# A second layer whose transposed onehot is compared from broadcast bytes, and gathers held to two groups in advance

## The reference

```
h = relu(layernorm(x))
x = x + segment_sum(h[src] @ weight[edge_type], dst)          # 16 edge types
h = relu(layernorm(x))
m = relu(concat(h[src], h[dst], edge_attr) @ W1 + b1) @ W2 + b2
x = x + segment_sum(m, dst)
```

## Time and profile before

| | |
|---|---|
| median of 3 runs | 5361.71 us (5358.94 to 5369.75) |
| the profiled execution | 5379.53 us, span 5377.8 us |
| mean granted clock of TensorE | 0.705 of 2.4 GHz |
| instructions | 53533 |

### The profile page before, as it was taken

The page is one execution under the profiler, slowest core; times in us unless marked ns, Lnnn a source line. Parts: engine busy times, 40 slices in busy tenths (PEclk is TensorE's granted clock), DMA queues, the critical chain, the costliest instruction groups (busy, mean ns, idle before and its releaser), DMA issues.

```text
span 5377.8 us, 53533 instructions
## 1 busy us (share of the span) xinstructions
PE 3005.4 (56%) x16541; PEld 2352.7 (44%) x16541; DVE 1166.7 (22%) x1424; ACT 742.7 (14%) x1550; POOL 3158.4 (59%) x3348
## 2 busy tenths in 40 slices
PE   2455555555555555555455566566556555565666
PEld 1333333333333333333345555455455555554555
DVE  5222222222222222222311111111111111111111
ACT  2111111111111111111111111111111111111111
POOL 7665665666666665665455555555555555555554
PEclk9677667676776776777767766666676777666667
DMA  4111111111111111111111111111111111111111
GB/s 94 22 25 22 24 25 22 24 25 23 24 25 23 25 23 23 25 24 23 23 24 27 27 27 27 26 27 26 26 27 26 28 27 27 26 27 26 26 28 24
DMA packets 248095, 144.20 MB, mean 27 GB/s; under 512 B 178526, under 2 KB 194199, under 8 KB 248071
## 3 DMA queue, kind: packets, MB, share of 16 engines
q0 software_dynamic: 106496, 109.26, 11.4%
q1 hardware_dynamic: 138949, 34.02, 3.1%
q10 hardware_dynamic: 2626, 0.63, 0.1%
HBM read 129.98 MB, written 12.83 MB: 27 GB/s over the span
## 4 chain that ended last, share of the span: by engine, by line
PE 44%; issue 32%; another core or an unknown queue 21%; DVE 1%; ACT 1%; SPq 1%; DVEq 0%; ACTq 0%; DMA 0%
PE ps L1278 9%; PE ps L1270 9%; PE ps L1202 7%; PE ps L1209 7%; PE ps L1261 4%; PE ps L1268 3%; PE ps L1216 2%; PE ps L1176 1%; PE ps L1249 1%; PE ps L1259 1%; ACT slots L803 0%; DVE onehot L977 0%; SPq L530 0%; PE ps L1165 0%
## 5 line engine op out<-in xcount | busy, mean ns | idle before, releaser
L648 POOL DMA_INDIRECT rows<-p_table,idx x1664 | 1569.9, 943 | 1203.1 <-DMA idx<-in_src_dram 655.6
L648 POOL DMA_INDIRECT rows<-h_table,idx x1616 | 1528.2, 946 | 974.3 <-DMA idx<-src_tab 497.5
L1270 PE MATMUL ps<-q_win,onehot_t 128*128 128x64 f32 x3328 | 579.7, 302 | 797.5 <-issue 795.8
L1270 PEld LDWEIGHTS ps<-q_win,onehot_t 128*128 128x128 f32 x3328 | 568.4, 232 | 932.7 <-issue 932.3
L1202 PE MATMUL ps<-onehot,rows 128*64 128x256 f32 x3328 | 709.3, 477 | 317.4 <-issue 310.0
L1209 PE MATMUL ps<-w_types,slots 128*128 128x128 f32 x3328 | 531.2, 316 | 437.1 <-issue 367.8
L1209 PEld LDWEIGHTS ps<-w_types,slots 128*128 128x128 f32 x3328 | 484.2, 226 | 498.1 <-issue 405.7
L1278 PE MATMUL ps<-onehot,relus 128*65 128x128 f32 x3328 | 575.5, 339 | 155.3 <-issue 110.8
L1202 PEld LDWEIGHTS ps<-onehot,rows 128*64 128x64 f32 x3328 | 337.5, 167 | 607.5 <-issue 530.1
L1278 PEld LDWEIGHTS ps<-onehot,relus 128*65 128x65 f32 x3328 | 511.0, 180 | 180.2 <-issue 164.7
L977 DVE TENSOR_TENSOR onehot<-key,ps 128x2048 f32<-128x2048 f32 x209 | 473.0, 2276 | 456.9 <-remote 441.7
(11 more groups left out here) (117 smaller groups left out, 1037.5 us busy)
## 6 DMA issues: line engine op xcount, KB each, us to landing
rows<-p_table,idx POOLq DMA_INDIRECT x1664
rows<-h_table,idx POOLq DMA_INDIRECT x1616
attr<-in_edge_attr_dram SPq DMA_DIRECT2D x209, 32.0 KB
q_win<-q_table SPq DMA_DIRECT2D x208, 32.0 KB
idx<-in_src_dram SPq DMA_DIRECT2D x208, 4.0 KB
idx<-src_tab SPq DMA_DIRECT2D x202, 4.0 KB
p_table<-pq_out SPq DMA_DIRECT2D x25, 120.0 KB
q_table<-pq_out SPq DMA_DIRECT2D x25, 120.0 KB
```

What stands on the lines that cost most here:

```text
L648: pool.indirect_dma_start(rows[:, u, t, :], None, table, bass.IndirectOffsetOnAxis(ap=idx[:, u, t:t + 1], axis=0)).then_inc(s, 16)
L1270: last = pe.matmul(pre_ps[:, u % 2, j * D:(j + 1) * D], onehot_t[:, u % 2, j * P:(j + 1) * P], q_win[:, u % V, :], start=False, stop=(j == ...
```

## The change

*Second layer, the transposed onehot.* Early on, DVE writes the keys of all edges within their group's window as bytes (`key_bytes`, capped at 255), and SP stores them in a DRAM table of 208 rows of 1024 bytes. In the second layer SP reads four rows at a time, broadcast to all 128 partitions (`key_rows`), and DVE compares a row with the partition's own number (`node_f`), which gives `onehot_t` in SBUF. PE's eight transposes and ACT's two copies of a group are gone; the transposed attributes stay.

*Second layer, loads and order.* Attributes come for four groups in one DMA, and `start_row` with its value loads is gone. SP has one wait for a group. `products(k-1)` comes ahead of the turn of group k on PE, and `add_window`, `add_rows` come ahead of the onehots on DVE. Several waits that others imply are left out.

*Both layers, POOL.* A second wait stands before each group's gathers: the sums (first layer) or row additions (second) of the group two back must be done.

```diff
+        key_table = dram("key_table", (G, GE), u8)
...
+            sp.dma_start(key_table.rearrange("(a g) e -> g a e", a=2), key_bytes[:]).then_inc(bytes_stored, 16)
...
+                def load_keys(g, k):
+                    rows_of = key_table[bass.ds(g, B), :].rearrange("(a g) e -> a g e", a=1)
+                    sp.dma_start(key_rows[:, k * B:(k + 1) * B, :], rows_of.broadcast_to([P, B, GE])).then_inc(key_in[k], 16)
+                def load_attr(g, k):
+                    sp.dma_start(attr[:, k * B:(k + 1) * B, :], attr_of(bass.ds(g * GE, B * GE))).then_inc(attr_in[k], 16)
...
+                def groups(it, ahead=2):
+                    for u in range(U):
+                        g = it * U + u
+                        wait_apart(sp, pre_added, AHEAD + g + 1)
+                        if ahead == 2 or ahead == 1 and u < U - 1:
+                            load_idx((g + U) * GE, u)
...
+                        if ahead or u < V:
+                            load_q(g + V, u % V)
+                        if u % B == B - 1 and (ahead or u < B):
+                            k = u // B
+                            load_keys((it + 1) * U + k * B if ahead else 0, k)
...
                         wait_apart(pool, idx_in[u], 16 * (it + 1) if u >= EG else 16 * it)
+                        wait_apart(pool, slots_summed, 2 * AHEAD + 2 * (it * U + u - 1))
...
                         wait_apart(pool, idx_in[u], 16 * (it + 1 + (NIT if u >= EG else NIT - 1)))
+                        wait_apart(pool, pre_added, it * U + u + AHEAD - 1)
...
-                    act.wait_ge(pre_made, AHEAD + g - 1)
                     act.copy(attr_t[0:T * F, b, :], attrt_ps).then_inc(turn_copied, 1)
-                    for half in range(2):
-                        cols = slice(half * 512, (half + 1) * 512)
-                        act.copy(onehot_t[:, b, cols], oht_ps[:, cols]).then_inc(turn_copied, 1)
...
+            dve.tensor_scalar(key_bytes[:].rearrange("g a (j p) -> g a j p", j=T), key1_g.rearrange("g a (p j) -> g a j p", j=T),
+                              float(2 * P - 1), None, ALU.min).then_inc(bytes_made, 1)
...
+                def make_onehots(g, it, u):
+                    dve.tensor_tensor(oh1[:, u % 4], key1[...], iota_ps[...], ALU.is_equal)
+                    if u % B == 0:
+                        dve.wait_ge(key_in[u // B], 16 * (it + 1))
+                    dve.tensor_scalar(onehot_t[:, u % 2, :], key_rows[:, u, :], node_f[:], None, ALU.is_equal).then_inc(onehot1, 1)
...
-                    for j in range(T):
-                        last = pe.transpose(oht_ps[:, j * P:(j + 1) * P], oh1[:, u % 4, j, :], ident[:])
-                    last.then_inc(group_turned, 1)
...
-                    turn_group(k, it, u)
                     if not first or u >= 1:
                         products(k - 1, it if u else it - 1, (u - 1) % U)
+                    turn_attr(it, u)
```

More of the change, by code:

```diff
@@ L38, in gnn_kernel @@
     V = 4
+    B = 4
     NIT = G // U
@@ L110, in gnn_kernel @@
         onehot_t = sb("onehot_t", [P, 2, T * P], fp32)
-        attr = sb("attr", [P, V, T * F], fp32)
+        attr = sb("attr", [P, U, T * F], fp32)
         attr_t = sb("attr_t", [T * F + 1, 2, P], fp32)
@@ L273, in gnn_kernel @@
         q_in = [sem(f"q_in_{u}") for u in range(V)]
-        attr_in = [sem(f"attr_in_{u}") for u in range(V)]
+        attr_in = [sem(f"attr_in_{h}") for h in range(U // B)]
+        key_in = [sem(f"key_in_{h}") for h in range(U // B)]
+        tail_in = sem("tail_in")
         onehot1 = sem("onehot1")
@@ L585, in _ @@
             with sp.If(fits > 0):
[L586 to L591, removed]
-                    base = sp.value_load(base_row[0:1, bass.ds(g, 1)], min_val=0, max_val=N - 1)
[L593 to L610, removed]
-                    for u in range(U):
-                        group(it, u)
-                    store_out(it - 2, chunk_nodes)
+                def attr_of(edges):
+                    return edge_attr[edges, :].rearrange("(g p j) f -> p g (j f)", p=P, j=T)
+                def load_keys(g, k):
+                    rows_of = key_table[bass.ds(g, B), :].rearrange("(a g) e -> a g e", a=1)
+                    sp.dma_start(key_rows[:, k * B:(k + 1) * B, :], rows_of.broadcast_to([P, B, GE])).then_inc(key_in[k], 16)
@@ new lines, in load_attr, with load_last_attr @@
+                def load_attr(g, k):
+                    sp.dma_start(attr[:, k * B:(k + 1) * B, :], attr_of(bass.ds(g * GE, B * GE))).then_inc(attr_in[k], 16)
+                def load_last_attr():
+                    first, k = (G - B) * GE, U // B - 1
+                    sp.dma_start(attr[:, k * B:U - 1, :], attr_of(slice(first, first + (B - 1) * GE))).then_inc(tail_in, 16)
+                    sp.wait_ge(tail_in, 16)
+                    sp.dma_start(attr[:, U - 1:U, :], attr_of(slice(LAST, E))).then_inc(attr_in[k], 16)
@@ new lines, in load_idx, with load_q @@
+                def load_idx(first, u):
+                    sp.dma_start(idx[:, u, :], src[bass.ds(first, GE)].rearrange("(p j) -> p j", j=T)).then_inc(idx_in[u], 16)
+                def load_q(g, v):
+                    base = sp.value_load(base_row[0:1, bass.ds(g, 1)], min_val=0, max_val=N - 1)
+                    sp.dma_start(q_win[:, v, :], q_table[bass.ds(base, P), :]).then_inc(q_in[v], 16)
+                def groups(it, ahead=2):
+                    for u in range(U):
+                        g = it * U + u
+                        wait_apart(sp, pre_added, AHEAD + g + 1)
+                        if ahead == 2 or ahead == 1 and u < U - 1:
+                            load_idx((g + U) * GE, u)
+                        elif ahead == 1:
+                            load_idx(LAST, u)
+                        if ahead or u < V:
[3 more added lines that the diff above has]
+                            load_keys((it + 1) * U + k * B if ahead else 0, k)
+                            if ahead == 2 or ahead == 1 and k == 0:
+                                load_attr((it + 1) * U + k * B, k)
+                            elif ahead == 1:
+                                load_last_attr()
@@ new lines, in _ @@
+                sp.wait_ge(bytes_stored, 16)
+                for k in range(U // B):
+                    load_keys(k * B, k)
+                    load_attr(k * B, k)
+                for v in range(V):
+                    load_q(v, v)
+                groups(0)
+                with sp.Fori(1, NIT - 2) as it:
+                    groups(it)
+                    store_out(it - 1, chunk_nodes)
+                groups(NIT - 2, ahead=1)
+                store_out(NIT - 3, chunk_nodes)
+                groups(NIT - 1, ahead=0)
@@ L1108, in step @@
                     k = it * U + u
[L1109 removed]
+                    if not first or u >= 2:
+                        add_window(k - 2)
+                    if not first or u >= 1:
+                        add_rows(k - 1, it if u else it - 1, (u - 1) % U)
+                    make_onehots(k + 1, it if u < U - 1 else it + 1, (u + 1) % U)
                     if not first and u == 7:
                         chunk_out(it - 1, chunk_nodes)
[L1112 to L1115 removed]
                 dve.wait_ge(prep_copied, 12)
[L1118 removed]
                 dve.memset(acc[:], 0.0).then_inc(z_added, AHEAD)
+                make_onehots(0, 0, 0)
                 for u in range(U):
```

60 lines of the change are left out of this document (26 added, 34 removed).

## The result

The changed kernel takes **5200.01 us** (median of 4 runs, 5183.84 to 5213.19) beside 5365.73 us for the kernel before in the same comparison (4 runs, 5358.94 to 5395.05): a ratio of 0.9672, 95% interval 0.9632 to 0.9712. That is 166 us faster; 237 were forecast. The profiled execution took 5183.84 us, span 5182.0.

What follows compares the result with a forecast made beforehand. It took PE's starvation during POOL's nonstop gathers, making index loads late, as the bound. Savings of 162 + 56 + 20 less 3 made 235 us, giving 5125 us; range 4850 to 5450.

Steps and rivals of the forecast that it cites:

- The second layer: Second layer without PE's eight transposes a group: 12.3 us a group instead of 13.08, -162 us.
- The other signs named ahead: Profile after: POOL waits of 4 to 5 us on sums or row additions, shorter layer gap, earlier first row addition.
- the gap: From the first layer's last gather to the second layer's first: -20 us, bounds 0 and -35.
- the budget of loads: While POOL gathers nonstop, PE gets about 60 weight loads, then about 1 a microsecond, until some 3 us after POOL pauses.
- The first layer's term (-56): First layer with POOL's new wait: 12.25 us a group against 12.52, over 208 groups, -56 us.
- The start (+3): Kernel start: one 104x2048 pass for key bytes and a small store, less the start row; +3 us at most.
- DVE's comparison: Second layer, 128x1024 bytes: 0.3 to 1.2 us a group; lengthening gathers by 0 to 0.7 us, taken as nothing.
- Key traffic at nothing: Second layer's larger broadcast key loads: price 0 to 1 us a group if gathers wait behind them, taken as 0.
- A, the hold starves the sums: Both layers: POOL's new waits leave PE's sums late, about 15.1 and 15.25 us a group; 6350 us, chance 0.2.
- B, PE never starves: Both layers: POOL's short stops keep the weight loads from running out; 11.3 us a group, 4740 us, chance 0.12.
- C, the hold does nothing: First layer stays at 12.52 us a group; only the second layer's removed transposes pay; about 5205 us, chance 0.2.
- D, no change: Loads don't count, or key traffic or DVE's lock takes PE's saving; 5361 less 16 to plus 10 us, chance 0.05.

Runs made afterwards that it cites:

- run 10: Kernel before with only POOL's two new waits added, the first from the 25th group on; chip 14: 5308.7 us, 0.9746 of the kernel before.
- run 9: Changed kernel with POOL's first-layer wait from the 25th group on instead of the 9th; chip 14: 5254.71 us, 0.9657 of the kernel before.
- run 5: The changed kernel again, unaltered, on chip 0: 4274.64 us, 1.0122 of the kernel before.
- run 8: Changed kernel with the byte comparison over one of eight tiles, output not the reference's; chip 0: 4245.06 us, 1.0048 of the kernel before.
- run 3: Changed kernel with eight identity transposes a group put back on PE, results unread; chip 5: 4266.23 us, 1.0118 of the kernel before.
- runs 7: Kernel before with only POOL's two new waits added; chip 0: 4243.66 us, 1.0045 of the kernel before.
- the pause: Changed kernel plus a POOL memset of 492 columns and a wait for it each group; chip 5: 4721.6 us, 1.1199; repeated, 4720.43 us, 1.1198.

## Why the prediction was right, and where it was not

**The second layer was right in size and in the shape of its cycle**: 12.3 us a group forecast, 12.27 measured, -162 us forecast, -165 measured. A cycle has 20 us of gathers, then 4.65 us in which PE comes back, the rows are added and POOL restarts, 24.6 for two groups. Loads fell to 36.1 a group. The other signs named ahead came too: a gap of 28.4 us (under 45 forecast), waits of POOL of 4.5 us, a first row addition 12.5 us after the layer's first gather (within 15 forecast; 45.6 us of waiting before), and a gather over 1 us beside the comparison.

**What pays in it was wrong in part, and that the term came out is partly luck.** The forecast booked the 162 us under PE's fewer loads. Its own cycle already had the hold in it, by the restart without an index load (some 1 us instead of 2.35), but it priced the hold at 76 us in all, 56 in the first layer and 20 in the gap. On chip 14 the hold alone brings 137 us. The rest of the change brings 54 us of the kernel and 57 of the second layer's gathers (2629.5 us from first to last in run 10, 2572.8 in run 9). POOL's stops show how. Before, 91 of 6.6 us in 187 groups, each with an index load behind the row addition; in run 10, 106 of 4.7 us in 181.5 groups; in run 9, 102 of 4.3 us in 185.9. So the stops are shorter with the hold, and with the rest of the change somewhat rarer and shorter again. The first figure is from another chip than the others, and how the 137 us divide between the layers isn't shown.

Nor is the budget of loads what ends PE's quick phase after the change. In the cycle shown no load was left over on the path: PE's sum had ended at 4013.87, and POOL waited for DVE, which got its signal at 4025.1. The change's own order, `add_window` ahead of `add_rows`, puts the row addition behind that signal, though its product (L1302) had ended at 4011.88. The changed kernel was not run with the other order.

**The first layer's term (-56) was mis-sized, in two ways.** The rate of 12.52 came from a stretch that ends at 2600 us, while the last gather starts at 2577; 23 us of the gap between the layers were counted in it. Without them it is 2377 / 191.75 = 12.40, and the term by the same argument (2.40 less 2.25, times 208) is 31 us. And the cycle of 12.25 came out at 12.33. Three of four stops in a turn of eight groups are 3.3 to 5.0 us (medians 3.9 to 4.0), at or under the 4 to 5 forecast, but the fourth, where a chunk of output is made, has a median of 8.8 and reaches 9.2:

```profile
1488.10 0.95 POOL L684 DMA_INDIRECT rows<-h_table,idx  x1 [0.30 <-issue]
1492.03 0.27 ACT L845 COPY nodes_t<-ps 128x128 f32<-128x128 f32 x1 [18.02 <-remote]
1492.26 0.59 ACT L802 COPY stage<-acc 64x480 f32 x1
...
1493.00 0.68 PE L1202 MATMUL ps<-ident,stage 64*120 64x64 f32 x4 [15.86 <-ACT stage L802]
1493.61 0.29 PEld L1239 LDWEIGHTS ps<-onehot,rows 128*64 128x64 f32 x4
...
1497.70 0.95 POOL L684 DMA_INDIRECT rows<-h_table,idx  x1 [8.65 <-PE ps L1239]
```

PE needs ACT's `stage` ahead of the next sum; ACT's copy starts only after POOL has stopped, and the whole sum follows it. The prediction costed the loads of a cycle, and not this trip from PE to ACT and back once in eight groups.

**The start (+3) left out the hold's first stop**: 27.8 us ahead of group 8 in the profile after (22.5 on chip 0). Gather 64 starts at 127 us where it started at 101. The 26 us less some 13 from the better rate are the +12.4 of the layer's last gather. POOL has at most two groups in advance instead of eight by then, so the gap after it is short (-30.4, forecast -20, inside its bounds). Taken together, start, first layer and gap bring 18 us; 73 were forecast. That is the missing part of the sum.

**The end** (-12.8) was not forecast. It is the same effect as in the gap: 14.8 us after the last gather instead of 27.6, as PE is at most two groups behind. 165.0 + 18.0 + 12.8 = 196, the difference of the spans.

**DVE's comparison.** Its time was bounded at 0.3 to 1.2 us; the rows below are of the profile after and of run 5 (min, median and max ns):

```profile
L1129 DVE TENSOR_SCALAR onehot_t<-key_rows,node_f x209: 742/745/974, 2623.9 to 5164.8; 128x1024 f32<-128x1024 uint8 x105
```

```profile
L1129 DVE TENSOR_SCALAR onehot_t<-key_rows,node_f x209: 741/905/997, 2150.9 to 4245.0; 128x1024 f32<-128x1024 uint8 x105
```

Its price to the gathers was bounded at 0 to 0.7 us a group. One gather beside it takes 1.11 or 1.14 us instead of 0.95, and the mean of all rises from 943 to 965 ns, 8 x 0.022 = 0.18 us a group. Each of the 209 comparisons in either trace overlaps a gather, so neither median is that of an undisturbed one. They differ with the place in the gather at which the comparison starts. In the profile after that is 0.24 us into it (median), the comparison takes 0.745 and most such gathers 1.11. In run 5 it is 0.51 us into it, the comparison takes 0.905 and the gather 1.02. The gathers grow by 158 ns a comparison in the first and 142 in the second, and 208 x 0.142 are the 30 us. Where POOL is the bound, run 8 shows them in the time. The Trainium skill, SBUF — State Buffer, "Who interferes with whom", says that a vector operation in a two-port mode shuts GpSimd out of a shared port; the lengthened gather agrees in its sign, but a gather loses some 0.16 us to an operation of 0.75, not the whole length that the start had suggested. That the comparison runs in such a mode isn't shown. Key traffic at nothing was right on chip 0 (run 8).

**The rivals.** *A, the hold starves the sums*, is refuted where it was meant: run 10 gains 2.5% from the hold alone. Of its two readings of the budget the count varies less than the time: over the second layer's runs of POOL, PE's quick phase (to the first 3 us with fewer than five loads) holds 61 loads in 8.7 us before, 63 in 10.9 after, 63 in 11.3 in run 9 and 59 in 9.7 in run 10 (medians). That settles little: after the change most runs of POOL have exactly 63, as the phase ends at one place of the program, the wait for ACT's copy. In the first layer it is 42 to 56 loads in 5.4 to 7.8 us, so neither is a constant. *B, PE never starves*, was wrong of the change, but it is just what chips 0 and 5 do with the kernel before. *C, the hold does nothing*, falls with run 10, though its 5205 us lies nearest to the median: its terms were wrong and its sum close by luck. For the first layer's rate it was near: 12.40 before, once read rightly, and 12.33 after. *D, no change*, falls as far as it goes: run 9 is 54 us faster than run 10. Whether loads are what counts in that isn't shown; the only run that kept them (run 3) was on a chip where POOL never stops. For chips where POOL never stops none of the cases holds, and the sign is the other.

**What stays open.** Why PE, SP and ACT starve beside POOL on one chip and not on another isn't shown. For the kernel before with the hold alone, gathers have the same length (944 ns in the second layer of runs 7 and 10) and spacing (0.30 us) on both kinds, the program is the same, and PE's clock doesn't explain idle PE. Chip 14 and the one of the first comparison may share something else than the chip: the runs can't tell a property of the chip from one of its surroundings at that hour. One thing in the traces does differ. The trace of run 5 records 72567 updates of semaphores, the profile after, of the same kernel, 20668. Of the 53248 that the landings of the gathers make (16 each), run 5 has 53230, the profile after 11935, that of before 10670 and run 10 11690. So where POOL stops long most updates are missing from the trace, and "waits for nothing that a row shows" is weak evidence there, in the prediction as well. It also leaves a rival that no run tests: that the recording of updates, and not the gathers themselves, is what holds the signals up. Not tried on a chip where POOL stops long: the changed kernel with the transposes kept, the bytes without the hold, and the pause, which would have been the direct test of whether any stop of POOL restores PE.

## What to carry to other kernels

Take the rate of a stage between its own first and last instruction, not from a round window, or the gap behind it is counted twice. When a producer is kept back, count where its lead was of use: the start gets a stop, the ends of the stages get shorter, and only the difference is a gain. And when a forecast rests on a slowness that no row explains, time both kernels on more than one chip before believing in it: this change was worth 3.3% in one comparison and cost 1.2% in another.

## What the runs showed of the hardware that was not expected

The same program took 4215 us on chip 5, 4224 on chip 0 and 5366 to 5446 us elsewhere, each steady within 0.7%. On the slower kind, after 9 to 11 us of gathers back to back, signals from PE to ACT and DVE are late: in run 9 half of the copies of `attr_t` start over 5 us after the transpose that they wait for ended by its record, up to 13.6 us, and mostly some 3 us after POOL's last gather has ended. In run 5, on chip 0, none of the second layer's starts over 4.5 us after it. Some of SP's issues take 0.71 us there where most take 0.34. On the other kind POOL makes over 1400 gathers without a long stop and PE does 3.5 loads a microsecond all the while. A one-source comparison of 128x1024 bytes into fp32 takes 0.745 us on DVE if it starts 0.24 us into a gather and 0.905 if it starts 0.51 us into it, and lengthens the gathers by 0.14 to 0.16 us in all.
